# A graph layer on one core: an earlier first scoring step, picks written to two places, and six sorted parts instead of five

## The reference, cut to what matters

```python
h_proj = jnp.einsum('nd,rde->rne', h, relation_weight)      # 32 relations
t_r = h_proj[etype, src]
h_r = h_proj[etype, dst]
att = jnp.sum(t_r * jnp.tanh(h_r + efeat), axis=-1)          # one score for each edge
seg_max = jax.ops.segment_max(att, dst, num_segments=N)
att_exp = jnp.exp(att - seg_max[dst])
denom = jax.ops.segment_sum(att_exp, dst, num_segments=N)
a = att_exp / denom[dst]
h_nb = jax.ops.segment_sum(h[src] * a[:, None], dst, num_segments=N)
out = leaky_relu((h + h_nb) @ res_w1.T) + leaky_relu(h * h_nb @ res_w2.T)
```

## Time and profile before

| what | us |
|---|---|
| median of 3 runs | 3904.87 (3899.4 to 3909.29) |
| profiled execution, its own time | 3897.68 |
| its span, first to last instruction | 3896.0 |
| VectorE busy | 2547.9 (65%) |
| GpSimd busy | 2846.5 (73%) |
| TensorE busy | 1908.0 (49%) |
| ScalarE busy | 1863.8 (48%) |

### The profile page before, as it was taken

How to read it: one execution, slowest core, us unless ns; L and a number is a source line. 1 busy time by engine, 2 the same in 40 slices (tenths; PEclk the granted TensorE clock), 3 DMA queues, 4 the chain that set the end, 5 groups by cost and what they waited for, 6 DMA issues and landing times.

```text
span 3896.0 us, 42532 instructions
## 1 busy us (share of the span) xinstructions
PE 1908.0 (49%) x10767; PEld 1495.1 (38%) x10767; DVE 2547.9 (65%) x5158; ACT 1863.8 (48%) x5179; POOL 2846.5 (73%) x4049
## 2 busy tenths in 40 slices
PE   5719997565556412222200003553555665766563
PEld 2206665454444312212200002433444544665553
DVE  9957774778787489999934233694787556444442
ACT  0008885567676557777601002212212224877773
POOL 8888884888888487888667777777777401878787
PEclk9969998556565555555555556766756785666665
DMA  6577775445454346666532224524444421212120
GB/s 236 223 265 241 268 262 184 128 153 164 153 168 147 125 156 208 214 210 205 162 77 73 80 68 135 149 67 139 134 120 131 136 82 37 70 55 63 53 63 21
DMA packets 261701, 548.06 MB, mean 141 GB/s; under 512 B 107792, under 2 KB 119930, under 8 KB 261462
## 3 DMA queue, kind: packets, MB, share of 16 engines
q1 hardware_dynamic: 179702, 445.68, 34.4%
q0 software_dynamic: 81760, 99.65, 10.3%
HBM read 275.18 MB, written 273.83 MB: 141 GB/s over the span
## 4 chain that ended last, share of the span: by engine, by line
POOL 38%; issue 14%; DVE 12%; PE 9%; ACT 6%; DMA 5%; POOLq 0%; SPq 0%; DVEq 0%; ACTq 0%
POOL arena L1353 20%; POOL result L1344 9%; DMA work<-slot_rows 4%; POOL slot_rows L1349 4%; POOL work L1353 3%; PE banks L1952 2%; POOL pause L1361 2%; DVE spare L950 1%; PE banks L1938 1%; PE banks L1981 1%; DVE spare L941 1%; ACT work L1535 1%; PE banks L2032 1%; ACT work L1524 1%; ACT work L1758 1%
## 5 line engine op out<-in xcount | busy, mean ns | idle before, releaser
L1344 POOL DMA_INDIRECT result<-work,outi x392 | 474.6, 1211 | 315.2 <-DVE work L1052 194.4
L1353 POOL DMA_INDIRECT work<-in_x,dsafe x392 | 438.6, 1119 | 112.7 <-POOL pause L1361 104.9
L1353 POOL DMA_INDIRECT arena<-g_by_node_and_edge,m_idx x392 | 433.4, 1106 | 116.2 <-POOL pause L1361 108.2
L1349 POOL DMA_INDIRECT slot_rows<-work,dsafe x392 | 386.3, 986 | 156.2 <-POOL pause L1366 66.1
L1353 POOL DMA_INDIRECT arena<-h_by_node_and_edge,m_idx x392 | 417.0, 1064 | 111.6 <-POOL pause L1361 60.0
L1843 PE MATMUL banks<-ident,work 128*128 128x128 f32 x392 | 96.6, 395 | 589.6 <-ACT arena L1506 543.4
L1353 POOL DMA_INDIRECT arena<-input_and_place_by_node,src_i x252 | 311.0, 1234 | 75.0 <-POOL pause L1361 73.0
L1843 PEld LDWEIGHTS banks<-ident,work 128*128 128x128 f32 x392 | 67.1, 208 | 610.9 <-issue 557.8
L1535 ACT ACTIVATE work<-work,q_stat 128x64 f32<-128x64 f32 x784 | 264.7, 428 | 0.9 <-DVE q_stat L624 0.9
L1524 ACT ACTIVATE work<-work,q_stat 128x64 f32<-128x64 f32 x784 | 260.3, 339 | 0.0
L1952 PE MATMUL banks<-work 128*128 x1112 | 201.3, 339 | 99.1 <-ACT work L1690 86.9
(11 more groups left out here) (339 smaller groups left out, 6778.7 us busy)
## 6 DMA issues: line engine op xcount, KB each, us to landing
slot_rows<-work SPq DMA_DIRECT2D x64, 834.0 KB, 8.2
work<-slot_rows SPq DMA_DIRECT2D x139, 384.0 KB
input_and_place_by_node<-arena SPq DMA_DIRECT2D x49, 528.0 KB, 3.1
g_by_node_and_edge<-arena SPq DMA_DIRECT2D x49, 512.0 KB, 5.4
arena<-x_of_destination SPq DMA_DIRECT2D x56, 448.0 KB, 4.2
work<-g_by_node_and_edge SPq DMA_DIRECT2D x49, 512.0 KB, 3.7
h_by_node_and_edge<-work SPq DMA_DIRECT2D x49, 512.0 KB, 2.7
work<-h_by_node_and_edge SPq DMA_DIRECT2D x56, 448.0 KB, 3.8
```

What stands on the lines that cost most here:

```text
L1344: pool.indirect_dma_start(out=table[:, :], out_offset=bass.IndirectOffsetOnAxis(ap=idx, axis=0), in_=of, in_offset=None, bounds_check=boun ...
L1349: pool.indirect_dma_start(out=table[:, :], out_offset=bass.IndirectOffsetOnAxis(ap=idx, axis=0), in_=of, in_offset=None).then_inc(signal, 16)
L1353: pool.indirect_dma_start(out=to, out_offset=None, in_=table[:, :], in_offset=bass.IndirectOffsetOnAxis(ap=idx, axis=0)).then_inc(signal, 16)
```

## The change

- `PART_STEPS` becomes `(0, 8, 15, 19, 22, 25, 28)`. Parts 0 and 1 are as before, part 2 has four steps instead of five, and parts 3, 4 and 5 have three steps each. Tiles are 144, 132, 88, 76, 76 and 76, that is 592 or 148 score groups.
- The planner lets part k begin in the first step of part k+1 (`>=`), charges 2.9 for a score group and 1.0 for a pick, and has a room of 30 for steps below 25 and 35 from there on.
- The two picks of an item write their by-product (`picked`, never read) to two places. Each then waits for the pick two before it, not for the one directly before it.
- The zeroing writes 1776 words at a time, still 64 times.

```diff
-PART_STEPS = (0, 8, 15, 20, 24, 28)
+PART_STEPS = (0, 8, 15, 19, 22, 25, 28)
...
-ZW = 1668
+ZW = 1776
...
-        picked = part(spare, S0, [KH], F16)
+        picked = [part(spare, S0, [KH], F16), part(work, 17536, [KH], F16)]
...
-                    for kind, cost, n in (("score", 2.6, PART_TILES[k] // RG), ("pick", 1.35, (PART_COLS[k][1] - PART_COLS[k][0]) // 2))]
+                    for kind, cost, n in (("score", 2.9, PART_TILES[k] // RG), ("pick", 1.0, (PART_COLS[k][1] - PART_COLS[k][0]) // 2))]
...
-                room = 31.0
-                while left and s > PART_STEPS[left[0][0] + 1] or left and s == GE:
+                room = 30.0 if s < PART_STEPS[-2] else 35.0
+                while left and s >= PART_STEPS[left[0][0] + 1] or left and s == GE:
...
-                    after(dve, pick["done"], 2 * i + c)
-                    stt(out=picked[:, 0:n], in0=tile_no[:, 0:n], scalar=tile_of[:, t:t + 1], in1=bank(5 + i % 2 * 2)[:, c * KH:c * KH + n],
+                    after(dve, pick["done"], 2 * i + c - 1)
+                    stt(out=picked[c][:, 0:n], in0=tile_no[:, 0:n], scalar=tile_of[:, t:t + 1], in1=bank(5 + i % 2 * 2)[:, c * KH:c * KH + n],
```

## The result

| | before | after |
|---|---|---|
| median of the timed runs, us (6 each) | 3903.03 (3899.4 to 3909.75) | 3939.76 (3926.38 to 3951.01) |
| ratio | 1 | 1.0098, 95% interval 1.0081 to 1.0114 |
| profiled execution, its own time | 3897.68 | 3937.71 |

The changed kernel is slower by 1.0%. The two profiled executions differ by 40.0 us, and all but 0.8 of it is inside the score stage: the stage starts at 1977.12 and 1978.14 us, and what follows the last pick takes 651.0 and 650.8.

What follows compares the result with a forecast made beforehand. VectorE's run of queued work was taken to bound the score stage's end. Terms -5 + 40 + 16 + 7 - 11 = +47 us, the walk +51, taken as +50: 3904.9 + 50 = 3955 us, range 3918 to 3982.

Steps and rivals of the forecast that it cites:

- What bounds: Score stage: GpSimd's sends set the pace up to about 2970 us; VectorE's run without waits from 2670 ends it at 3245.00.
- Earlier start: Score stage, parts 0 and 1: scoring starts a send sooner, beside sends that passed with VectorE idle; -5 us.
- The walk: Step-by-step timing of the score stage, all 21 steps, with sends that can be delayed: +51 us.
- the head start: By the scan of step 18, 20 groups of part 1 done instead of 11: worth nine groups, eaten by nine extra ones.
- Placements: Score steps with sorting: 32 placements each in steps 20 and 23 cost more than the old spread; net 40 us.
- The two full steps: Steps 20 and 23, each placing all 32 relations of a part: 69.4 and 67 us.
- The sign to look for: Scans of steps 21 and 22, and 24 and 25, some 65 to 70 us apart, VectorE nearly without idle time between.
- Six parts: Score stage: 148 groups instead of 139, nine more costing 27 us at 3.05, eating the head start.
- Picks: VectorE's picks in the score stage: two places gain 0.08 us each, times 140, -11 us.
- Zeroing: First 280 us: 3.5 MB more zeroed, 15 us if all exposed; taken as 0, as nothing waits behind.
- The tail shrinks: Rival, behind the last scan: 14 fewer picks, one group more, -15 us, nothing else matters; 3890 us, chance 0.11.
- Groups become slower: Rival, score groups: 3.3 us instead of 3.05, 92 groups cost 23 us more; 3978, chance 0.12 for this or more.

Runs made afterwards that it cites:

- e7: The changed kernel with four parts (0, 8, 15, 21, 28) and ZW 1572, rest as changed: 3881.21 us, ratio 0.9943 to the kernel before.
- e2: The changed kernel with the five parts and the zeroing of before, rest as changed: 3884.09 us, ratio 0.9941 to the kernel before.
- e8: The kernel before with only the scoring of a part starting a step sooner (>= in the planner): 3892.25 us, ratio 0.997.
- e1: The changed kernel with both picks writing to one place again and waiting for the pick before: 3967.14 us, ratio 1.0156 to the kernel before.
- e3: The kernel before with only the two places for the picks' by-product: 3890.37 us, ratio 0.996.
- e5: The changed kernel with parts 4 and 5 counted a step earlier, their placements spread over two steps: 3950.59 us, ratio 1.0119 to the kernel before.

## Why the prediction was right

- **What bounds.** Right for the kernel before, the changed one and the variants with five and six parts. In e7 the last send sets the end (43.68 us of waiting), and in e2 the run has a wait of 9.29 us for it. The stages behind kept their length (648.5 to 652.1 us).
- **Earlier start.** The walk put the third group of part 0 at 2354, the scans of steps 10, 16, 17 and 18 at 2381, 2595, 2663 and 2706. They stand at 2355.72, 2382.49, 2596.79, 2661.86 and 2710.03. Groups are scored beside sends that used to pass idle. The scan of step 18 is where it was (2710.39), so the term of -5 us came to nothing. That the nine extra groups eat the head start is borne out by the 92 groups that both kernels have behind it, and by e8, where the start without more groups is a gain.
- **Placements.** The two full steps were forecast at 69.4 and 67 us and took 69.9 and 66.9. Their price was read from the rows of one placement. The sign to look for, VectorE nearly without idle time, was too strong: it was busy for 84% and 88%. The last send was forecast near 3170 and went out at 3153.75.
- **Six parts.** e2 confirms the sign; no run splits the terms. The parts had +40, +16 and +7 for placements, steps that begin with groups, and counts: 63. The run of the changed kernel grew by 40.5, and with the 12 of the picks given back by 53.
- **Picks.** Forecast 11 us in the run; by e1's steps 12. Here the sum was right by luck and its makeup wrong: 0.08 for all, where wide ones gain 0.12 to 0.17 and narrow ones 0.04 to 0.06. The wide ones were sized by a row of the closing step. The Trainium skill, page "VectorE: DVE Perf Modes", section "The DRAIN you can't avoid", has a semaphore between this engine's operations cost nothing, shown with copies. e3's step 19 (26.05 against 29.97 us) contradicts that for this pair of instructions.
- **Zeroing.** 0 as taken: the stage's start moves by 1.0 us, inside its spread over executions.
- **Rivals.** "The tail shrinks" is right as a part, 16.2 us against 15, but the full steps decided. "Groups become slower" falls: in the closing step one group follows the next by 2.81 us before and 2.80 after (3151.71 to 3210.82 for 21 distances, 3209.89 to 3260.23 for 18). Over all profiles the same distance is 2.8 to 3.1 us in the six kernels with 556 tiles and 2.8 to 3.0 in the three with 592.

**Where the 12 us went.** The run was to grow by about 52 and grew by 40.5. Put together from the prediction's own prices, it comes to about 585 us and took 575.1. Three terms were mis-sized:

- *A wide pick.* 1.10 us was taken and 0.97 measured in step 18. Steps 18 and 19 with the 49 wide picks took 37.9 and 36.9 instead of 41.5 and 39.9: 6.6 us.
- *Placements beside groups.* A group was taken at 3.45 us where 16 placements stand among ten, and took 3.9 in step 17 ((50.0 - 9.3 - 1.8) / 10) and in step 16. There the third group came at 2677.09, as forecast, and the eight from it to the scan at 2710.03 took 33 us instead of 29. So step 17 lies 4.4 us on the other side, and step 16 ate most of the head start of 5 us.
- *The pace of a plain group.* 3.05 us was worked out from one step at one clock (0.85) with a placement in each group. It fits step 21 (39.4 us for 39.8) and not step 24 (36.1, or 2.7 a group). The two steps have the same items; the granted clock was 0.67 and 0.82.

The third group of step 16, and the windows of steps 18, 21 and 24:

```profile
2677.09 0.42 DVE L904 TENSOR_TENSOR dsti<-banks,work 128x256 f32<-128x256 f32 x1 [3.30 <-PE banks L1952]
...
2760.04:2797.96 37.92, 20.00 (x199) 15.83 (x199) 29.11 (x122) 6.25 (x10) 29.85 (x53) 0.82 0.25 73
...
2904.77:2944.20 39.43, 24.17 (x120) 21.64 (x120) 15.61 (x33) 12.78 (x23) 27.83 (x51) 0.67 0.57 157
...
3053.21:3089.27 36.06, 20.16 (x116) 16.59 (x116) 15.58 (x33) 13.10 (x23) 15.36 (x28) 0.82 0.53 161
```

In e1 step 24 took 38.0 us at 0.75, between the two. Step 18 does not show the clock's part: in e1 it took 41.3 us at 0.58, but its 21 picks with one place explain the whole difference. The walk over all steps, which I preferred to the plain sum by 4 us, carried the same prices and was further off than the sum.

## What to carry to other kernels

Work that is slipped into an engine's idle time has a price that depends on its neighbour. Here one placement of 1.5 us in each score group mostly fits into the group's idle time (11 groups and 11 placements took 43.6 us), while a second in a group mostly adds to it (ten groups alone took 39.4 us, with 32 placements 69.9) and one beside picks costs in full (1.5 us in e2). So before splitting work into more parts, count the idle room where the fixed cost of each part will lie. A change made of several edits should be timed edit by edit: two of these gained 16 and 14.5 us, and the third hid them by costing about 56. Price an instruction by a row of its own width and neighbours.

## What the runs showed of the hardware

- On VectorE a wait on the engine's own previous instruction, where the accumulator is read in between, costs 0.12 us behind the start of that read in the closing step, 0.04 to 0.06 a pick when picks of 76 to 104 tiles follow each other, and 0.17 with 132 tiles (0.12 where the counts stand between them).
- The accumulator read is hidden entirely once nothing waits for it: it starts at 3265.75, and so does the next pick.
- The pace of the score groups, a loop whose steps on TensorE and VectorE wait for each other, went with TensorE's granted clock. Ten groups and nothing else took 36.1 us at a mean of 0.82, 38.0 at 0.75 and 39.4 at 0.67 (1 is 2.4 GHz). In the groups of the last part, one followed the next by 2.8 us at 0.90 to 0.97 (before, after, e8) and by 2.9 to 3.1 at 0.81 to 0.87 (the other seven). Closing stretches of equal work took 153.9 us at 0.75 and 162.5 at 0.69 (e5), and 163.5 at 0.70 in e1, of which 1.4 are its picks. What set the clock in each execution stays open.
